# A causal filter bank as fp32 matmuls: the first 64 columns of two filter blocks as 64-row tiles side by side

## The reference, cut to what matters

```
U_plus  = causal convolution of t with each of 16 filters phi[:, k] (length 784)
U_minus = the same with the signs of odd tokens turned, there and back
out     = sum over k of sigma[k]^0.25 * (U_plus[k] @ Mpp[k] + U_minus[k] @ Mpm[k])
out    += t @ Mu[0] + t shifted by 1 @ Mu[1] + t shifted by 2 @ Mu[2]
```

## Time and profile before

| | |
|---|---|
| median of 3 runs | 381.0 us (380.25 to 381.39) |
| the profiled execution | 378.57 us |
| its span, first to last instruction | 376.6 us |
| PE busy | 348.6 us, 93% of the span |
| DVE, ACT, POOL busy | 222.4, 176.4, 19.8 us |
| mean granted TensorE clock | 0.991 of full |
| filter, mixing and direct matmuls on the chain | 270.36 to 371.74 us |

### The profile page before, as it was taken

The page is one execution under the profiler, slowest core; times in us unless marked ns, Lnnn a source line. Parts: engine busy times, 40 slices in busy tenths (PEclk is TensorE's granted clock), DMA queues, the critical chain, the costliest instruction groups (busy, mean ns, idle before and its releaser), DMA issues.

```text
span 376.6 us, 11555 instructions
## 1 busy us (share of the span) xinstructions
PE 348.6 (93%) x5075; PEld 203.8 (54%) x5075; DVE 222.4 (59%) x329; ACT 176.4 (47%) x168; POOL 19.8 (5%) x40
## 2 busy tenths in 40 slices
PE   8898999999999998698899998578799999999995
PEld 7435557744333346473463344344566666676784
DVE  1878999999999986555747766155321212121112
ACT  3852997888898931434547766213211111111110
POOL 4490000000000011000000000000000000000000
PEclk9999999999999999998999999899999999999999
DMA  5617200000000009000000000000310000000001
GB/s 165 216 21 263 83 3 0 2 2 3 2 2 2 2 5 337 18 16 2 0 2 2 2 2 0 0 2 0 87 44 4 3 3 3 3 2 3 5 3 44
DMA packets 10185, 12.80 MB, mean 34 GB/s; under 512 B 4102, under 2 KB 8984, under 8 KB 10136
## 3 DMA queue, kind: packets, MB, share of 16 engines
q1 hardware_dynamic: 9160, 8.85, 7.7%
q0 software_dynamic: 832, 3.00, 2.4%
q10 hardware_dynamic: 144, 0.20, 0.2%
HBM read 10.44 MB, written 0.40 MB: 29 GB/s over the span
## 4 chain that ended last, share of the span: by engine, by line
PE 79%; DVE 6%; issue 4%; ACT 4%; DMA 2%; SPq 1%; DVEq 0%; ACTq 0%
PE PS L917 79%; ACT pool_ L425 2%; DVE RSC L534 1%; DMA W1R<-in_fwa 1%; DMA W4R<-in_aw 1%; DVE pool_ L861 1%; DVE TMP L723 1%; DVE pool_ L751 0%; DVE pool_ L575 0%; ACT pool_ L445 0%; ACT SDC L340 0%; ACT H1P L371 0%; DVE X L766 0%; DVE TMP L764 0%; SPq L252 0%
## 5 line engine op out<-in xcount | busy, mean ns | idle before, releaser
L917 PE MATMUL PS<-pool_,CON 128*32 128x392 f32 (+2 forms) x1320 | 110.2, 492 | 0.6 <-DVE pool_ L751 0.4
L398 ACT ACTIVATE pool_<-TMP,WA 128x3136 f32<-128x3136 f32 x27 | 78.1, 2925 | 12.2 <-PE PS L917 11.4
L917 PEld LDWEIGHTS PS<-pool_,CON 128*32 128x32 f32 (+1 forms) x1320 | 49.5, 110 | 59.2 <-issue 46.4
L751 DVE TENSOR_SCALAR pool_<-TMP,WA 128x3136 f32<-128x3136 f32 x45 | 81.3, 1848 | 0.1
L905 DVE COPY pool_<-PS 128x392 f32<-128x392 f32 x32 | 18.1, 567 | 83.3 <-PE PS L917 83.3
L494 ACT ACTIVATE pool_<-PS 128x392 f32<-128x392 f32 x32 | 15.9, 498 | 85.0 <-PE PS L917 85.0
L917 PE MATMUL PS<-HE,WS 128*32 128x136 f32 (+3 forms) x1024 | 46.3, 333 | 0.8 <-DVE WS L900 0.8
L917 PE MATMUL PS<-pool_,WS 128*32 128x392 f32 (+3 forms) x1024 | 46.3, 333 | 0.0
L917 PEld LDWEIGHTS PS<-HE,WS 128*32 128x32 f32 x1024 | 31.4, 111 | 16.3 <-issue 10.0
L917 PEld LDWEIGHTS PS<-pool_,WS 128*32 128x32 f32 x1024 | 32.0, 110 | 14.8 <-issue 8.6
L917 PE MATMUL PS<-CON 128*128 128x196 f32 (+2 forms) x208 | 37.0, 322 | 1.2 <-DVE QZ L567 0.5
(11 more groups left out here) (222 smaller groups left out, 295.4 us busy)
## 6 DMA issues: line engine op xcount, KB each, us to landing
pool_<-in_pho SPq DMA_DIRECT2D x1, 3144.0 KB, 12.0
HE<-in_phe SPq DMA_DIRECT2D x1, 3136.0 KB, 11.7
QZ<-CW SPq DMA_DIRECT2D x12, 98.0 KB, 2.2
CW<-in_cw POOLq DMA_DIRECT2D x2, 576.0 KB, 4.7
CON<-in_con POOLq DMA_DIRECT2D x1, 732.5 KB, 5.8
out_y<-Y SPq DMA_DIRECT2D x1, 392.0 KB, 2.4
CQ<-in_ws SPq DMA_DIRECT2D x16, 9.0 KB
MPP<-in_mpp POOLq DMA_DIRECT2D x1, 256.0 KB, 3.0
```

Source lines behind the costliest of these rows:

```text
L398: a.activation(RING[:, g % RG, :, :].rearrange("p b (r c) -> p b r c", r=SIDE), window(n // CQ), ACT.Abs, bias=WA2[:, n:n + 1], scale=-1.0 ...
L751: v.tensor_scalar(RING[:, g % RG, :, :].rearrange("p b (r c) -> p b r c", r=SIDE), window(n // CQ), WA2[:, n:n + 1], None, ALU.max).then_i ...
L917: return t.matmul(out_, lhsT, rhs, start=start, stop=stop, skip_group_check=True)
```

## The change

Two blocks u0 and u0 + 1 are now written together. Where before every matmul used all 128 rows, four short pieces of a pair use 64:

- upper(u): output columns 0 to 63 of piece 0, from partitions 64 to 127 alone.
- lower(u): output columns 128 to 191, the first 64 of piece 1, from partitions 0 to 63 alone. For that, piece 1 of the input has its two halves exchanged when it is turned into UT, and the strips that it meets are loaded a second time with their halves exchanged (SWE for even taps; SWO and SWP for odd taps, in the loop's free buffers and in S2P).
- whole(u): all that is left, with all 128 rows: 328, 200, 136 and 8 columns.

upper of one block and lower of the other stand next to each other. They use different rows of the array and different banks. The core of the diff:

```diff
+            for q, at in ((0, 64), (64, 0)):
+                sp.dma_start(SWE[q:q + 64, :, :], bass.AP(phe.tensor, at, [[1, 64], [LE, NK], [1, SWN]])).then_inc(s["sw_in"], 16)
+            for q, at in ((0, 64), (64, 0)):
+                sp.dma_start(SWO[q:q + 64, :, :], bass.AP(pho.tensor, at, [[1, 64], [LO, SWK], [1, SWN + 1]])).then_inc(s["sw_in"], 16)
+                sp.dma_start(SWP[q:q + 64, :, :], bass.AP(pho.tensor, SWK * LO + at, [[1, 64], [LO, NK - SWK], [1, SWN + 1]])).then_inc(s["sw_in"], 16)
             sp.wait_ge(s["ln_out"], 8)
...
-                    last = mm(PS[:, 4 + c, P * i:P * i + P], URV[:, a0:a0 + 255:2], con_("ident"))
+                    if i == 1:
+                        mm(PS[0:64, 4 + c, P:2 * P], URV[:, a0 + P:a0 + P + 127:2], con_("ident"))
+                        last = mm(PS[64:128, 4 + c, P:2 * P], URV[:, a0:a0 + 127:2], con_("ident"))
+                    else:
+                        last = mm(PS[:, 4 + c, P * i:P * i + P], URV[:, a0:a0 + 255:2], con_("ident"))
...
+            t.wait_ge(s["sw_in"], 96)
...
+                def upper(u, start):
+                    for kk in range(4):
+                        mm(PS[32 * kk:32 * kk + 32, u % 6, 0:64], UT[64:128, 4 * c, 32 * (u % 4):32 * (u % 4) + 32],
+                           plain(4 * g + kk)[64:128, 0:64], start, False)
+
+                def lower(u, start):
+                    for kk in range(4):
+                        last = mm(PS[32 * kk:32 * kk + 32, u % 6, P:P + 64], UT[0:64, 4 * c + 1, 32 * (u % 4):32 * (u % 4) + 32],
+                                  turned_half(4 * g + kk)[0:64, 0:64], start, False)
+                    return last
+
+                def whole(u):
+                    for i in range(4):
+                        skip = 64 if i < 2 else 0
+                        n = NPH - P * i
+                        for kk in range(4):
+                            k = 4 * g + kk
+                            last = mm(PS[32 * kk:32 * kk + 32, u % 6, P * i + skip:NPH], UT[:, 4 * c + i, 32 * (u % 4):32 * (u % 4) + 32],
+                                      (turned_half(k) if i == 1 else plain(k))[:, skip:n], False, False)
+                    return last
+
+                for u in (u0, u0 + 1):
+                    if u >= 6:
+                        t.wait_ge(s["uev_act" if u % 2 == 0 else "uev_dve"], (u - 6) // 2 + 1)
+                upper(u0, True)
+                lower(u0 + 1, True).then_inc(s["halves"], 1)
+                whole(u0)
+                t.wait_ge(s["halves"], u0 // 2 + 1)
+                upper(u0 + 1, False)
+                lower(u0, False).then_inc(s["u_done"], 1)
+                whole(u0 + 1).then_inc(s["u_done"], 1)
```

More of the change, by code:

```diff
@@ L44 @@
 LE, LO = NPH + 127, NPH + 128
+SWN, SWK = NPH - P, 13
 MAGIC = 12582912.0
@@ L140, in build @@
         UT = WS2[:, 0:8, :]
+        SWE = arena[:, 4 * T:4 * T + NK * SWN].rearrange("p (k t) -> p k t", k=NK)
+        SWO = arena[:, 4 * T + NK * SWN:4 * T + NK * SWN + SWK * (SWN + 1)].rearrange("p (k t) -> p k t", k=SWK)
+        SWP = S2P[:, 0:(NK - SWK) * (SWN + 1)].rearrange("p (k t) -> p k t", k=NK - SWK)
         KEYS = Y1; QT_ = QZ[:, 0, :]
@@ L212, in build @@
             "wmx_part wmx_rows wmx_row wmx_bc q_sc q_chain cq_chain cq_done x2_ready q_xin cc_done cv_relu cv_q x3_ready x3_sum "
-            "wexp w_fill w_soft u_mixed w_chain sg_ready d_chain d_ready lags_in ut_done ut_ready urv_ready u_done uev_act uev_dve mix_done y_ready stored"
+            "wexp w_fill w_soft u_mixed w_chain sg_ready d_chain d_ready lags_in sw_in halves ut_done ut_ready urv_ready u_done uev_act uev_dve mix_done y_ready stored"
         ).split()}
@@ L1224, in _, with filtered, plain, turned_half @@
             t.wait_ge(s["strip_in"], 32)
-            def filtered(u):
-                grp, b = u // 4, u % 4
+            t.wait_ge(s["sw_in"], 96)
+            def filtered(u0):
+                grp = u0 // 4
                 g, a2, odd = grp // 4, (grp // 2) % 2, grp % 2
                 c = a2 ^ odd
[L1231 to L1234, removed]
-                    for kk in range(4):
[L1236 to L1243, removed]
+                off = odd * a2
+                def plain(k):
+                    return HO[:, k, off:] if odd else HE[:, k, :]
+                def turned_half(k):
+                    if not odd:
+                        return SWE[:, k, :]
+                    return (SWO[:, k, off:] if k < SWK else SWP[:, k - SWK, off:])
+                def upper(u, start):
+                    for kk in range(4):
+                        mm(PS[32 * kk:32 * kk + 32, u % 6, 0:64], UT[64:128, 4 * c, 32 * (u % 4):32 * (u % 4) + 32],
[24 more added lines that the diff above has]
+                whole(u0 + 1).then_inc(s["u_done"], 1)
@@ L1256, in _ @@
             for grp in range(16):
-                for b in range(4):
-                    filtered(4 * grp + b)
+                filtered(4 * grp)
+                filtered(4 * grp + 2)
                 if grp:
```

## The result

| | before | after |
|---|---|---|
| median of 4 runs each, us | 380.76 (380.25 to 381.39) | 394.83 (389.67 to 395.41) |
| profiled execution, us | 378.57 | 395.41 |
| its span, us | 376.6 | 393.5 |
| its mean granted clock | 0.991 | 0.974 |

The ratio is 1.0339, with a 95% interval of 1.025 to 1.0427. A ratio compares the runs of both kernels without those over 1.5% above the fastest of their kernel, and so differs a little from that of the medians. The forecast was 393.7 us, so the kernel became slower by about as much as predicted. The profiled execution is also one with a low clock, and that share of the difference has to be taken out before the terms are compared.

What follows compares the result with a forecast made beforehand. PE was taken to bound the filter stage. 12.1 us there plus 0.6 for the turn made 12.7 on the profiled 378.6 (391.3), or 393.7 on the runs' median of 381.0; range 386.5 to 400 us.

Steps and rivals of the forecast that it cites:

- The price of a change: Filter blocks: each stretch with its own tile shape costs a fixed 0.14 us, whatever its length, as the array is emptied.
- whole stretches: Filter blocks' 128-row remainder: 1.185 us of columns plus 0.125 for the shape, 1.310 us each.
- One sign: Timeline of the changed filter stage: a group of four blocks should take 6.35 us instead of 5.59.
- Rival B: Filter blocks: half-height tiles have a smaller price, near 0.09 us; 386.3 up to 390 us; chance 0.12.
- rival A: Filter blocks: changing 128 to 64 rows within the same column groups needs no emptying; 376.7 us, faster; chance 0.07.
- Side by side: Shared 64-row stretches: both blocks' tiles run concurrently, saving 0.107 us each, 6.8 us over 64 stretches.
- shared stretch: Filter blocks, two blocks' 64-row pieces: 0.107 us of columns, 0.14 for shape, 0.03 for tile starts, 0.277 us.
- Rival C: Shared stretches: 64-row tiles don't overlap with four column groups each; another 6.8 us, 400.5 us; chance 0.07.
- The turn: Turn of the input before the filter stage: four changes of shape at 0.14 us, 0.6 us on the chain.
- The strips: Six added loads: 16.6 us by bytes, 24 by pieces, ending at 258 to 265 us, hidden before PE asks at 270.4.
- rival D: Added strip loads run at half of HO's rate, ending at 274 us, 4 us late: 397.5 us; chance 0.04.
- The clock: PE's granted clock over the kernel: PE stays at work for over four fifths of the time, so no effect.

Runs made afterwards that it cites:

- kernel without overlap: Changed kernel with every 64-row piece in a stretch of its own, four tiles and nothing beside it, 128 such stretches instead of 64: 416.83 us, ratio 1.0977.
- kernel with full rows: Changed kernel with its order, loads and waits, but all 128 rows used in the short pieces, zero halves computed again: 386.4 us, ratio 1.0149.
- a quarter of the changes: Changed kernel with all 64-row pieces of a four-block group in one stretch ahead of the four whole pieces: 388.88 us, ratio 1.0187.
- 7 pieces: Kernel before, each block cut into 7 instead of 4 matmuls per filter, same columns, all 128 rows: 398.31 us, ratio 1.0492.
- half as many changes: Changed kernel with the 64-row pieces of two pairs sharing one stretch at either end of a four-block group: 387.69 us, ratio 1.0217.
- 10 pieces: Kernel before, each block cut into 10 instead of 4 matmuls per filter, same columns, all 128 rows: 440.5 us, ratio 1.1603.

## Why the prediction was right, and where it was not

**The price of a change.** This was the weakest step, taken from attention's 32-row tiles, and it held: 0.14 us for a stretch of its own shape with four tiles (0.139 in the kernel without overlap), 0.12 for a long one, and 7 ns for each further tile. A change of rows alone costs what a change of rows and columns costs in the earlier trace rows. That the sum came out within 0.1 us of the measurement is closer than either is known: the whole stretches were a little overrated (1.310 for 1.305, 0.3 us in all), the turn a little underrated. One sign came out otherwise: a group of four blocks should have taken 6.35 us, and took 6.21. The mixing behind the fourth block has tiles of the same shape, so the array is emptied behind the mixing, which takes 0.80 us to the next block for 0.68 before. From group to group, 7.01 us, the sum holds. The rule of the Trainium skill (TensorEngine Tiling (Array Packing), section Tiling Modes) that a change of tiling mode drains the engine agrees with the runs: each change costs 0.12 to 0.14 us, whatever the number of columns. Rival B's smaller price and rival A are refuted by the same stretches.

**Side by side.** The first convolution in the earlier trace rows was the right witness: the two sets of four start 0.02 us apart, and the shared stretch takes 0.273 us, where one after the other would be 0.38. Rival C is out. The 6.8 us that the overlap should save are there. They are outweighed by 64 x (0.166 + 0.12) = 18.3 us of price; the difference, 11.5, is what the stage shows within 0.2.

**The turn.** 0.7 us for 0.6, in an execution at the full clock.

**The strips.** In the changed kernel, from 236 to 290 us (busy tenths and GB/s of the DMA engines in 40 slices, then issues with KB each and us to landing):

```profile
DMA  0000038999999999999999100666743300000000
GB/s 0 0 0 0 0 11 237 195 194 192 214 196 193 192 207 194 192 195 206 192 189 190 35 0 0 149 149 165 177 109 70 86 0 0 12 0 12 0 0 12
...
pool_<-in_phe SPq DMA_DIRECT2D x2, 1056.0 KB, 10.7
pool_<-in_pho SPq DMA_DIRECT2D x2, 861.2 KB, 16.7
```

They keep the engines busy from about 243 to 266 us. That is 23 us, close to my bound by pieces (24), and not the 16.6 us by bytes. It ended about a us after the window that I gave, and well before PE asked. The cover was there; it was thinner than the middle of my estimate. That the bound by pieces fitted is partly luck. By bytes the loads ran at 190 to 200 GB/s, half of what the load of HO reached (last section), so the condition of rival D came true. Its 33 us were too many, because they doubled a time from issue to landing: HO's 12.0 us hold only about 8 in which data moved. At 195 GB/s, 4.33 MB take 22 us. (By bytes the prediction should also have had 16.2 us: HO's 3144 KB are 3.22 MB.) The reciprocal that ran during them and is on the chain still took 1.39 us (264.99), as in the earlier trace rows.

**The clock.** "Nothing" was right as a cause and wrong for a single execution. The profiled ones differ by 16.9 us and not by 12.6, since that of the changed kernel had more stretches at half clock, which the kernel before has too in other executions. The medians of four differ by 14.1 us, for the same reason: three of the changed kernel's four runs had clocks of 0.974 to 0.982.

**What failed: rival A's price.** I wrote that without emptying the kernel would take 376.7 us. That left out that the additional matmuls and their weight loads are also instructions that PE has to be given. A group of the changed kernel has 96 matmuls of two passes and 32 mixing passes, each with a weight load: 448 instructions, for 320 before. At 14.4 ns they need 6.45 us, and a group took 6.27 before. So even at no price for the shape a group could not be faster than before; with the turn that is 16 x 0.18 + 0.7, some 3.6 us slower. The kernel with full rows bears it out: no changes of shape in the blocks, and 5.5 us slower at equal clock. Of these, 0.7 are the turn and 0.6 the 6.31 us groups; the rest, some 4 us, are waits for instructions. As it is, the changed kernel's group of 7.01 us has room for its instructions, and none of its 12.6 us comes from the feed. No run had the saved columns without the price, so this stays an estimate; by it the forecast stands, but its rival on the faster side did not exist, at any price of a change.

It also speaks against a better version of the same idea with as many matmuls. Merging the stretches can remove at most the price, and at 6.45 us a group the feed stands above the 6.27 of before. The kernels with a half and a quarter of the changes meet it, the second with its own waits on halves besides. None of the kernels tried beats the kernel before; one with fewer instructions was not tried.

## What to carry to other kernels

Count a stretch of tiles with another height as 0.14 us, plus some 0.12 us for going back, before counting the columns that it saves: here 64 fp32 columns saved 0.107 us, less than half of that. When work is cut into more and shorter matmuls, also count instructions: where a long run of matmuls and weight loads comes to less than 14.4 ns each, PE waits for its own program. With four fp32 tiles at once that is below 8 x 14.4 / 0.833 = 138 columns on average by these figures (it was 200 before, 114 with 7 pieces). And compare such kernels at the same granted clock; 0.01 of it was 2.8 us here, a quarter of the effect.

## What the hardware did that I had not expected

**PE's instructions come at a limited rate.** PE and PEld records in 300 to 370 us, with the packets of the instruction queue in the same time:

| kernel | PE + PEld | packets | ns each | PE busy, us |
|---|---|---|---|---|
| before | 3643 | 14 | 19.2 | 70.00 |
| changed | 4520 | 18 | 15.5 | 70.00 |
| half as many changes | 4684 | 19 | 14.9 | 69.13 |
| a quarter of the changes | 4709 | 18 | 14.9 | 69.11 |
| full rows | 4741 | 19 | 14.8 | 68.73 |
| 7 pieces | 4865 | 19 | 14.4 | 65.11 |
| 10 pieces | 4857 | 19 | 14.4 | 48.75 |

The waits begin where the mean falls below about 15 ns. Short bursts go much faster: the 16 matmul passes of a shared stretch and their 16 weight loads start within 0.13 us (288.84 to 288.97). This fits a store of instructions that is refilled in packets of 256, one each 3.68 us at best. The packets themselves are short: 1.8% of the 16 engines' 70 us are 20.2 us for 19 of them, 1.06 us each. With 10 pieces they never overlap; one starts about 1.2 us after a wait of PE has ended, and the next wait ends about 1.3 us after it is through. So most of the 3.68 us is the way around a packet, and not its transfer. Why no second one is under way meanwhile, no run shows.

**Waiting on one's own matmul.** A wait on a semaphore that PE raises itself is met 0.34 to 0.37 us after the start of the matmul that raises it (287.89 to 288.23, and 288.02 to 288.39), where that matmul's record is 0.22 us long. With 16 passes in between, 0.21 us of the first one were idle. A piece of work of a us or so in between hides it, as in the changed kernel.

**DMA of half the partitions.** The new strips move 190 to 200 GB/s with the engines busy for nine tenths, where the load of HO, in the kernel before between 134 and 160 us, reaches twice that at the same busy share:

```profile
DMA  0000000000669999999999993000022200100000
GB/s 0 0 0 0 0 0 0 0 0 0 58 152 392 380 397 389 392 405 365 375 387 372 377 375 121 24 17 0 25 6 65 79 15 0 38 0 0 0 0 0
```

The new loads differ in two ways, 64 partitions instead of 128 and pieces of 1056 or 1060 bytes instead of 1572. The pieces alone would explain a third less. Which of the two makes the rest was not tested.
